# A fused decoder layer on one NeuronCore: the end of its recurrence in another order

## What is computed

```python
def gla(x):                        # 16 heads, 8 key and 16 value dimensions
    q, k, v = x @ Wq, x @ Wk, x @ Wv
    gk = log_sigmoid(x @ Wgk1 @ Wgk2 + bgk2) / 16
    for t in range(1024):
        h = h * exp(gk[t]) + k[t] (outer) v[t]
        o[t] = (q[t] * 8 ** -0.5) @ h
    o = o * rsqrt(mean(o * o) + eps) * gnw * silu(x @ Wg)
    return o @ Wo
def xattn(x, ctx, idx):            # 16 heads, 64 indices per token
    q, c = x @ W_q.T, ctx @ W_kv_down.T
    k, v = split(c[idx] @ W_kv_up.T)
    return softmax(q k / 4) v @ W_out.T
x = layernorm(x + gla(x))
x = layernorm(x + xattn(x, ctx, idx))
x = layernorm(x + ffn(x))          # causal attention and 8 experts, top 2
```

## Time and profile before

| | |
|---|---|
| median of 3 runs | 1341.63 us (1338.9 to 1342.21) |
| profiled execution, its own time | 1336.39 us |
| span of that execution | 1334.6 us |
| PE busy | 1249.0 us, 94% |
| DVE busy | 927.3 us, 69% |
| ACT busy | 637.7 us, 48% |
| POOL busy | 243.2 us, 18% |
| mean granted clock of TensorE | 0.981 of full speed |

### The profile page before, as it was taken

The page is one execution under the profiler, slowest core; times in us unless marked ns, Lnnn a source line. Parts: engine busy times, 40 slices in busy tenths (PEclk is TensorE's granted clock), DMA queues, the critical chain, the costliest instruction groups (busy, mean ns, idle before and its releaser), DMA issues.

```text
span 1334.6 us, 19363 instructions
## 1 busy us (share of the span) xinstructions
PE 1249.0 (94%) x7665; PEld 932.9 (70%) x7665; DVE 927.3 (69%) x1435; ACT 637.7 (48%) x957; POOL 243.2 (18%) x273
## 2 busy tenths in 40 slices
PE   8674689998999999999999999999999999999997
PEld 6332367677655555568878888888888888888886
DVE  6999577877898989667677565555556556465657
ACT  6796744465487888863243333323323233233233
POOL 5777541005133433110000000000000000000000
PEclk9888899999999999999999999999999999999999
DMA  8766001015412222111000121101102011010001
GB/s 221 153 131 137 6 17 22 1 63 180 135 49 60 54 67 80 33 66 46 17 17 1 32 74 32 58 12 44 43 14 70 18 34 55 9 47 9 1 17 48
DMA packets 44939, 72.59 MB, mean 54 GB/s; under 512 B 10064, under 2 KB 27136, under 8 KB 44848
## 3 DMA queue, kind: packets, MB, share of 16 engines
q1 hardware_dynamic: 39664, 60.45, 16.6%
q0 software_dynamic: 3648, 10.09, 2.6%
...
## 4 chain that ended last, share of the span: by engine, by line
PE 53%; DVE 2%; ACT 0%; issue 0%; ACTq 0%; DVEq 0%
PE PS L2580 25%; PE PS L2593 25%; PE PS L2343 1%; PE PS L114 0%; PE PS L2606 0%; PE PS L2324 0%; PE PS L2357 0%; DVE OT_all L2741 0%; DVE r_st L2419 0%; DVE r_on L2436 0%; DVE r_on L2416 0%; PE PS L2618 0%; DVE X L2428 0%; DVE x_mid L2732 0%; ACT X L2702 0%
## 5 line engine op out<-in xcount | busy, mean ns | idle before, releaser
L2663 ACT ACTIVATE x_g<-PS,x_bias 128x512 f32<-128x512 f32 x256 | 175.9, 687 | 493.0 <-PE PS L2580 492.9
L2580 PE MATMUL PS<-x_h,x_w 128*128 128x512 f32 x1536 | 398.7, 395 | 0.0
L2593 PE MATMUL PS<-x_mid,x_w 128*128 128x512 f32 x1488 | 383.9, 393 | 1.1 <-DVE x_w L2315 1.1
L2580 PEld LDWEIGHTS PS<-x_h,x_w 128*128 128x128 f32 x1536 | 286.1, 188 | 64.5
L2593 PEld LDWEIGHTS PS<-x_mid,x_w 128*128 128x128 f32 x1488 | 279.2, 188 | 65.9 <-DVE x_w L2315 1.6
L2732 DVE CAST x_mid<-x_g 128x512 fp32r<-128x512 f32 x256 | 109.3, 427 | 266.4 <-ACT x_g L2663 266.0
L2182 DVE TENSOR_REDUCE a_M<-PS 128x2 f32<-128x1024 f32 (+1 forms) x144 | 173.1, 1223 | 24.4 <-PE PS L1879 18.2
L2734 DVE TENSOR_TENSOR x_mid<-x_g,x_mid 128x512 fp32r<-128x512 f32 x256 | 177.2, 692 | 8.8
L2120 ACT ACTIVATE f_parts<-PS 128x512 f32<-128x512 f32 x224 | 120.9, 601 | 36.5 <-PE PS L1933 25.0
...
L236 POOL TENSOR_TENSOR qh<-qh,QT 128x1024 f32<-128x1024 f32 x32 | 75.3, 2366 | 41.9 <-DVE qh L546 41.6
L546 DVE TENSOR_TENSOR_SCAN qh<-decay,PS 128x1024 f32<-128x1024 f32 x32 | 73.0, 2280 | 7.6 <-PE PS L342 6.8
...
## 6 DMA issues: line engine op xcount, KB each, us to landing
...
```

What stands on the lines that cost most here:

```text
L2580: last = e.matmul(PS[:, f % 2, :], w1[n % 2][u][:, kt, f * P:(f + 1) * P], self.rows(v, k)[:, kt, :], start=m == 0 and kt == 0, stop=m == ...
L2593: last = e.matmul(PS[:, 2 + 2 * (it % 2) + d, :], w2[n % 2][v][:, f, d * P:(d + 1) * P], mid[u][:, f % RM, :], start=f == 0 and m == 0, st ...
L2663: e.activation(g[s % RG][:, :], PS[:, f % 2, :], ACT.Gelu, bias=b1[:, n, f:f + 1]).then_inc(A.sem, 1)
```

## The change

Nothing is computed otherwise; lists are reordered, and two signs go from one engine to another.

- POOL makes six signs, 11, 19, 27, 35, 43, 51, and not the first four; 43 stands behind output 20 and 51 behind output 22. ACT makes two fewer. `out_gated_pool(0)` goes from behind output 23 to behind 24, `out_gated_pool(1)` from behind 24 to behind 27.
- DVE: the weights' low part goes from column 26 to column 24, ahead of both reciprocals, which now stand together there; the statistics of part 0 from column 29 to column 30; `out_rstd(0)`, the keys' low part and the value blocks from ahead of `state(31)` to behind it. The statistics of part 1 leave this block for the start of the next.
- PE: `counts` 10 and 12 to 16 are later by a step or more; "udc" follows "wqo" directly, and the product of part 0 follows its turn with only `counts(13)` between, and is not cut in two by counts. `c_turn` comes ahead of the product of part 1, `c_q` in the middle of it.
- ACT: the copies "wqo" ahead of the first root; signs spread anew; the masked key copies ahead of `out_copy(1)`; the halves of X ahead of the logarithm (L832); "y" of part 1 later.

```diff
--- before.py
+++ after.py
@@ -225,7 +225,7 @@
...
 
-        pooled = (11, 19, 27, 35)
+        pooled = (11, 19, 27, 35, 43, 51)
         of_scalar = lambda first, last: [n for n in range(first, last) if n not in pooled]
...
@@ -277,13 +277,13 @@
...
         output(e, jj)
-        if jj in (4, 7, 10, 15):
+        if jj in (4, 7, 10, 15, 20, 22):
             if jj == 4:
                 e.wait_ge(A.sem, A.at("idx"))
-            indicator(pooled[(4, 7, 10, 15).index(jj)])
-        elif jj == 23:
+            indicator(pooled[(4, 7, 10, 15, 20, 22).index(jj)])
+        elif jj == 24:
             self.out_gated_pool(e, 0, s_gate)
-        elif jj == 24:
+        elif jj == 27:
             self.out_gated_pool(e, 1, s_gate)
...
@@ -445,8 +445,8 @@
...
     sums(4)
+    turn(4)
     counts(10)
-    turn(4)
     e.wait_ge(s_tok, 10)
...
@@ -454,7 +454,6 @@
...
     weights_turned(self.wout, 5).then_inc(S.sem, 1)
-    counts(12)
     e.wait_ge(A.sem, A.at("wqo"))
...
@@ -463,6 +462,7 @@
...
     last.then_inc(S.sem, 1)
+    counts(12)
     e.wait_ge(A.sem, A.at("udc"))
...
@@ -470,18 +470,17 @@
...
     last.then_inc(S.sem, 1)
-    counts(13)
     e.wait_ge(A.sem, A.at("ckv"))
     self.out_turn_pooled(e, 0, SB, s_gate)
-    counts(14)
+    counts(13)
     e.wait_ge(A.sem, A.at("wo"))
     self.out_product(e, 0, SB, (0, 1))
-    counts(15)
     self.out_product(e, 0, SB, (2, 3))
-    counts(16)
+    counts(14)
     e.wait_ge(self.OA[0].sem, self.OA[0].at("y"))
...
     turn(6)
+    counts(15)
     e.wait_ge(s_tok, 14)
...
@@ -489,6 +488,7 @@
...
     last.then_inc(S.sem, 1)
+    counts(16)
     e.wait_ge(s_fin, 1)
...
@@ -496,14 +496,14 @@
...
     self.out_turn_pooled(e, 1, SB, s_gate)
-    self.out_product(e, 1, SB, (0, 1))
-    self.out_product(e, 1, SB, (2, 3))
     e.wait_ge(self.s_row, 1)
...
     self.c_turn(e, 0)
+    self.out_product(e, 1, SB, (0, 1))
+    self.c_q(e, 0, 2)
     e.wait_ge(self.VL.sem, self.VL.at("none"))
     sums(7)
-    self.c_q(e, 0, 2)
+    self.out_product(e, 1, SB, (2, 3))
     turn(7)
...
@@ -590,26 +590,22 @@
...
         elif jj == 24:
-            self.out_reciprocal(e, 0)
-        elif jj == 25:
-            self.out_reciprocal(e, 1)
-        elif jj == 26:
             e.wait_ge(A.sem, A.at("wqo"))
...
             e.tensor_tensor(flat_w(W[1][:, :, :]), PS[:, 4, :], flat_w(W[0][:, :, :]).bitcast(F32), ALU.subtract).then_inc(VC.sem, 1)
+            self.out_reciprocal(e, 0)
+            self.out_reciprocal(e, 1)
         elif jj == 30:
-            self.out_rstd(e, 0)
-            e.wait_ge(A.sem, A.at("khi"))
-            e.tensor_tensor(kT[1].bitcast(F32R), PS[:, 5, 0:2 * P], kT[0], ALU.subtract).then_inc(V.sem, 1)
-            e.wait_ge(self.C.sem, self.C.at("half_b"))
-            for b in range(B):
-                last = e.tensor_tensor(Vblk[:, b, :, :, :].rearrange("p a c d -> p a (c d)"),
-                                       PS[:, 4, b * D:(b + 1) * D].rearrange("p (a n) -> p a n", a=H // 2),
-                                       self.half[:, :, :].rearrange("p c d -> p (c d)").unsqueeze(1).broadcast_to((P, H // 2, 2 * HD)), ALU.mult)
-            last.then_inc(V.sem, 1)
-        elif jj == 29:
             self.out_stats_stored(e, 0)
-
+    self.out_rstd(e, 0)
+    e.wait_ge(A.sem, A.at("khi"))
+    e.tensor_tensor(kT[1].bitcast(F32R), PS[:, 5, 0:2 * P], kT[0], ALU.subtract).then_inc(V.sem, 1)
+    e.wait_ge(self.C.sem, self.C.at("half_b"))
+    for b in range(B):
+        last = e.tensor_tensor(Vblk[:, b, :, :, :].rearrange("p a c d -> p a (c d)"),
+                               PS[:, 4, b * D:(b + 1) * D].rearrange("p (a n) -> p a n", a=H // 2),
+                               self.half[:, :, :].rearrange("p c d -> p (c d)").unsqueeze(1).broadcast_to((P, H // 2, 2 * HD)), ALU.mult)
+    last.then_inc(V.sem, 1)
     e.wait_ge(self.c_cnt.sem, self.c_cnt.at("turn"))
...
@@ -622,7 +618,6 @@
...
     last.then_inc(VL.sem, 1)
-    self.out_stats_stored(e, 1)
     self.c_q_parts(e, 0, *self.qT0, 2)
...
@@ -782,22 +777,21 @@
...
     tokens(4, 0)
-    signs(46, 47)
     tokens(4, 1)
-    signs(47, 50)
+    signs(46, 49)
     silu(3, 4)
-    signs(50, 52)
-    self.out_root(e, 0)
+    signs(49, 50)
     e.wait_ge(S.sem, S.at("wqo"))
...
     e.activation(WoutT[:, :, :].rearrange("p k n -> p (k n)"), PS[:, 5, :], ACT.Copy).then_inc(A.sem, 1)
+    self.out_root(e, 0)
     self.out_root(e, 1)
+    signs(50, 53)
     e.wait_ge(S.sem, S.at("udc"))
...
     e.activation(self.Wo[:, :, :], self.Wo[:, :, :], ACT.Copy, scale=gnw[:, 0:1]).then_inc(A.sem, 1)
-    signs(52, 53)
     sums_out(5, 0)
...
@@ -809,34 +803,37 @@
...
                  ACT.Copy).then_inc(A.sem, 1)
-    signs(56, 58)
+    signs(56, 57)
     self.out_copy(e, 0, SB)
-    signs(58, 65)
+    signs(57, 62)
     self.out_stored(e, 0, SB)
+    signs(62, 63)
     sums_out(6, 0)
...
     tokens(6, 0)
+    signs(63, 64)
     tokens(6, 1)
+    signs(64, 65)
+    self.out_deviation(e, 0)
     e.wait_ge(S.sem, S.at("kv"))
...
     e.activation(self.cntT[:, :], wide(6), ACT.Copy).then_inc(s_fin, 1)
-    self.out_deviation(e, 0)
-    self.out_copy(e, 1, SB)
     e.wait_ge(A.sem, A.at("khi"))
...
     last.then_inc(self.AC.sem, 1)
+    self.out_copy(e, 1, SB)
+    self.c_x1(e, 0)
     e.wait_ge(self.VL.sem, self.VL.at("least"))
     e.activation(lc, lc, ACT.Ln).then_inc(self.AL.sem, 1)
-    self.c_x1(e, 0)
-    self.out_stored(e, 1, SB)
+    self.c_q1(e, 0, self.qT0[0], 2)
     sums_out(7, 0)
     sums_out(7, 1)
+    self.out_stored(e, 1, SB)
     tokens(7, 0)
     tokens(7, 1)
-    self.c_q1(e, 0, self.qT0[0], 2)
 
...
@@ -1395,6 +1392,7 @@
...
     self.out_means(e, 2)
+    self.out_stats_stored(e, 1)
     maximum(0, 0)
...
```

## The result

| | before | after |
|---|---|---|
| first comparison, median (executions) | 1340.45 us (4) | 1322.08 us (4) |
| all executions with a clock on record, median, range | 1340.68 us, 1336.0 to 1344.9 (53) | 1323.3 us, 1321.6 to 1325.8 (8) |
| profiled execution, its own time | 1336.39 us | 1321.62 us |
| span | 1334.6 us | 1319.9 us |
| mean granted clock, that execution | 0.981 | 0.984 |

The ratio is 0.9866, with an interval from 0.9847 to 0.9885: 18.0 us faster, between 15.4 and 20.5. The forecast was a gain of 13.2, to 1328.4. Between the two profiled executions the difference is 14.8. The 53 do not hold the four of the first comparison, whose clocks are not on record; with them the median is the same. A repetition of the changed kernel gave a ratio of 0.9877 (0.9855 to 0.9898), 16.5 us: the two intervals overlap.

What follows compares the result with a forecast made beforehand. DVE's columns were taken to bound the first block, with two waits to remove. Terms -13.95 to sums(6), +0.5 tail and +0.2 next block gave -13.2 us off the median 1341.63: 1328.4 us, range 1324.0 to 1335.0.

Steps and rivals of the forecast that it cites:

- What bounds it: First block: DVE sets the pace at 3.65 us a column; it idles 6.79 ahead of state 27, 7.55 ahead of the statistics.
- Low part at column 24: DVE's low part earlier: sums(5) at 126.5, state 27 at 131.7 for 138.05, 6.35 us earlier, its wait gone.
- Turn and product: Part 0 on PE: turn at 134.05, product at 136.2, sums(6) at 142.6 for 156.55, 13.95 us earlier.
- rival 1: Half clock in the product of part 0: gain only 9.5, 1332 us, or between if partial; chance 0.27.
- Tail: From sums(6) to the block's end: signs +0.6, masked copies +1.0, turn of X -1.1; net +0.5 us.
- Next block: Statistics of part 1 ahead of the next block's two maxima on DVE: +0.2 us.
- POOL's signs: Two more signs on POOL, 3.63 us each, costed at nothing, with 3.9 us of cover at output 23.
- the rival by the shared port: POOL's signs stop DVE ahead of the low part, 7.3 us later: 1336 us; chance 0.04.
- Rivals 3 and 4: Half clock through tail and next block, 1351 us, chance 0.03; gain given back in a new wait, 1338 to 1345, chance 0.03.
- I take the gain off the median: Whole kernel: 13.2 us off the median 1341.63, which lies 5.2 above the profiled execution, giving 1328.4 us.
- clock term: TensorE's clock at sums(5): if it never dropped, these are 1.5 us shorter, -14.7 in all.

Runs made afterwards that it cites:

- The low part with its counts alone: Kernel before with DVE's low part at column 24, ACT's weights copy ahead of the roots, and counts(12) behind the third weight's turn: 1333.4 us, ratio 0.9949.
- split: Changed kernel with 5 of ACT's 8 masked copies ahead of the copy of part 1 and 3 behind the logarithm: 1322.1 us, ratio 0.9869.
- before filled: Kernel before with 4 idle matmuls ahead of the product of part 1 and 8 for 5 at the block's end: 1339.0 us, ratio 0.9995.
- low part alone: Kernel before with DVE's low part at column 24 and ACT's weights copy ahead of the roots, counts(12) not moved: 1335.1 us, ratio 0.9959.
- old tail in the changed kernel: Changed kernel with the order of PE's and ACT's steps in the tail as before: 1325.2 us, ratio 0.9886.
- filler at the low part: Changed kernel with 12 idle matmuls on PE ahead of its wait for the low part: 1323.7 us, ratio 0.9872.
- four signs: Changed kernel with four signs on POOL as before, ACT making 43 and 51 again: 1323.7 us, ratio 0.9877.
- split, statistics later: Changed kernel with masked copies 5 and 3, the next block's statistics of part 1 behind part 2's gating, and square(3) ahead of deviation(1): 1324.1 us, ratio 0.9877.
- outputs apart: Changed kernel with the piece from part 0's turn to the keys and values as before, counts between and inside: 1328.7 us, ratio 0.9903.
- statistics back: Changed kernel with the statistics of part 1 back at the end of DVE's list of the first block: 1326.5 us, ratio 0.9898.

## Why the prediction was wrong

**What bounds it** was right: two separate waits of DVE, each with its chain behind it. The low part with its counts alone took the first away and left the second.

**Low part at column 24:** turn at 123.31 (said 123.4), sums(5) at 126.42 (126.5), state 27 at 131.19 (131.7). What I had not priced is that counts(12) must move, too (the change moves them): with them in the old place the turn came at 127.8.

**Turn and product:** turn at 133.61 (134.05), product at 135.96 (136.2), sums(6) at 143.47 (142.6), because the clock was at half at the product's start: rival 1, in part, with 1.0 of its 3.7 us. In the second trace of the changed kernel the product ran at full clock, so it is not this order alone that brings it. So 13.1 for 13.95 here.

**Tail:** said +0.5, was -0.7 against the first trace of before (25.49 from sums(6) to the first scores for 26.18), and -1.0 against the old tail with everything else equal. The masked copies do cost their 1.0, as the split shows; so what I had too low must be the gain of X's turn and the product with W_q ahead of the last sums, which no run took apart.

**Next block:** said +0.2; the turn of part 2 starts at 177.91 for 191.73, 13.8 earlier, as the first scores. It cost nothing on this trace. **POOL's signs:** nothing, as said; the rival by the shared port did not show, DVE's states being 2.23 to 2.29 us next to them. Rivals 3 and 4 did not come.

**The sum on the trace** then is 13.8 us at the start of the next block, for 13.2 said. That it comes so near is partly luck: the middle gave 0.9 less than its term, the tail 1.2 and the next block 0.2 more. Over the span it is 14.7; the last 0.9 is what is left of gains and losses between 320 and 600 us (the lead is 16.2 us near 380), where no instruction was moved and the low stretches of the clock lay differently in the two traces.

**The step that failed** is "I take the gain off the median". I read the 5.2 us between the profiled execution of before and the median of three, 1341.63, as a constant that both kernels carry. For the profiled execution the forecast was 1323.2 us, and it took 1321.62, 1.6 less. The other 4.7 of the 6.3 us between 1328.4 and 1322.08 are this term: the changed kernel's median lay 0.5 above its profiled execution in the first comparison and 1.7 over all eight, and not 5.2.

Part of it is the small sample: over 53 executions the median of before is 1340.7, 4.3 above the profiled one and not 5.2. Most of the rest goes with the clock. The profiled execution ran at 0.981, the best that this kernel reaches. The median execution of before spent 61.6 us at half clock, the profiled one 50.7; at 0.32 us each, the slope over the 53 executions, these 10.9 us are 3.5 of the 4.3. For the changed kernel the two are 42.3 and 42.2: nothing, and its 1.7 lie in something that the mean clock does not show. Between the kernels the same slope gives an estimate only, since it was measured within one: 19.3 us between the medians are 6.2 us of time, 8.5 between the profiled two are 2.7, so 3.5 of the gain stand in the medians and not in the pair. Measured, the gain between medians is 18.4 in the first comparison, 17.3 over all executions and 16.5 in the repetition's series, for 14.8 in the profiled pair: 1.7 to 3.6 more. The prediction's clock term had allowed for -1.5 at sums(5), and for none in the stretches where the median execution differs from the profiled one.

Half-clock time in all 14 traces, in us, in three stretches: from 100 us to sums(6), the 38 us behind that, and from there to 600 us (for each slice of 2.5 us, twice (1 - granted clock) times its length, summed):

| kernels | to sums(6) | 38 us behind | to 600 us |
|---|---|---|---|
| before, and again | 20.4, 23.9 | 3.4, 10.2 | 3.4, 10.2 |
| before filled; low part alone; with counts | 23.8; 27.4; 13.7 | 3.4; 3.4; 10.2 | 6.8; 6.8; 10.2 |
| old tail in the changed kernel | 13.7 | 3.4 | 6.9 |
| changed, and again | 17.1, 10.3 | 0.0, 0.9 | 3.5, 5.9 |
| filler at the low part; four signs; split | 10.3; 17.1; 10.3 | 0.0; 0.0; 0.0 | 6.8; 6.8; 3.4 |
| split, statistics later | 10.2 | 4.8 | 5.4 |
| outputs apart; statistics back | 17.1; 13.6 | 6.8; 6.8 | 6.8; 6.8 |

It fell in two places. Ahead of sums(6) the traces with the old middle have 20 to 27 (13.7 for the one with the counts behind the turn), those with the new one 10 to 17. Behind sums(6) the six traces with the old tail have 3.4 to 10.2 and five of the eight with the new one 0 to 0.9. The other three show that the tail's order alone does not decide it. Ahead of 100 us all fourteen have 17.0 to 20.5. These are single traces of kernels whose executions differ among themselves by up to 7 us in one stretch (3.4 and 10.2 for before). Which wait of PE draws the half clock, and how often, stays open: filling one in the tail of the kernel before gave no shift clear of noise, and with one filled in the changed kernel the low stretch stood elsewhere. And the line through the executions says how time and clock go together, not that the clock is all of it.
